# Moving one of the three rotary products of a fused attention kernel from VectorE to GpSimd

## The reference, cut to what matters

```python
def rotate_half(x):
    d = x.shape[-1] // 2
    return jnp.concatenate([-x[..., d:], x[..., :d]], axis=-1)
# NH = 16 heads of HD = 16; cos and sin of position x frequency
q, k = q * cos + rotate_half(q) * sin, k * cos + rotate_half(k) * sin
ctx = sdpa(q, k, v, causal=True)
```

## Time and profile before

| | |
|---|---|
| median of three runs | 522.23 us (522.04 to 524.18) |
| profiled execution | 521.07 us, of which the span is 518.9 us |
| granted TensorE clock, mean | 0.963 |
| PE busy | 435.7 us (84%) |
| DVE busy | 353.8 us (68%) |
| ACT busy | 257.0 us (50%) |
| POOL busy | 152.0 us (29%) |
| the cosine products, L1072 on DVE | 16, 10.9 us |
| the q adds, L251 on POOL | 16, 13.3 us |
| chain that ended last | PE 59%, DVE 18%, ACT 7%, issue 5%, DMA 5%, POOL 4% |

### The profile page before, as it was taken

One profiled execution on the slowest core, in us unless ns is written; L12 is line 12 of the kernel. 1 busy time (PEld: TensorE's weight loads), 2 busy tenths in 40 slices (PEclk: granted clock), 3 DMA queues, 4 the chain that ended last, 5 costly groups with the idle time before them and its releaser, 6 DMA issues.

```text
span 518.9 us, 10981 instructions
## 1 busy us (share of the span) xinstructions
PE 435.7 (84%) x3842; PEld 337.3 (65%) x3842; DVE 353.8 (68%) x804; ACT 257.0 (50%) x726; POOL 152.0 (29%) x268
## 2 busy tenths in 40 slices
PE   1098669997899999999999999999997986898992
PEld 1076538675577777776776776776866875676771
DVE  5934468797698698698699599699682650535543
ACT  0356456663554564464464564464451432655662
POOL 3585233113123123113114114013012103446542
PEclk9999958999999999999999999999997997999996
DMA  7587763633103103103103103001004001112111
GB/s 244 187 283 237 250 243 129 197 126 123 32 20 95 42 11 104 42 1 113 42 1 113 42 3 113 25 18 52 9 4 142 22 20 51 32 51 69 54 42 41
DMA packets 29492, 44.44 MB, mean 86 GB/s; under 512 B 4224, under 2 KB 22528, under 8 KB 29440
## 3 DMA queue, kind: packets, MB, share of 16 engines
q1 hardware_dynamic: 25792, 31.12, 18.4%
q0 software_dynamic: 3648, 12.62, 7.4%
HBM read 27.34 MB, written 16.38 MB: 84 GB/s over the span
## 4 chain that ended last, share of the span: by engine, by line
PE 59%; DVE 18%; ACT 7%; issue 5%; DMA 5%; POOL 4%; POOLq 0%; SPq 0%; ACTq 0%; DVEq 0%
PE xyz L1444 6%; PE xyz L1485 5%; DVE E L1094 4%; PE xyz L1471 4%; PE b_ps L1598 4%; DVE mx L1092 4%; PE b_ps L1361 3%; PE b_ps L1362 3%; PE b_ps L1363 3%; POOL x_rows L1277 3%; PE xyz L1648 2%; PE xyz L1361 2%; PE xyz L1362 2%; PE xyz L1363 2%; PE xyz L1553 2%
## 5 line engine op out<-in xcount | busy, mean ns | idle before, releaser
L1092 DVE TENSOR_REDUCE mx<-xyz 128x8 f32<-128x512 f32 x64 | 43.8, 684 | 13.9 <-PE xyz L1444 13.7
L1094 DVE TENSOR_TENSOR E<-xyz,mx 128x512 f32<-128x512 f32 x64 | 44.3, 692 | 2.2
L1444 PE MATMUL xyz<-kT,qT 32*64 32x128 f32 (+1 forms) x768 | 44.3, 333 | 1.7
L1471 PE MATMUL xyz<-cst,E 128*128 128x128 f32 x256 | 37.2, 283 | 5.7 <-ACT E L787 2.8
L1598 PE MATMUL b_ps<-w_gu_hi,ms_hi 128*128 (+2 forms) x90 | 38.0, 422 | 3.9 <-ACT ms_hi L811 3.9
L1314 POOL TENSOR_TENSOR mvar<-mss,pow_eps 128x1 f32<-128x1 f32 x17 | 3.2, 188 | 121.2 <-ACT m_sqr L803 119.2
L1471 PEld LDWEIGHTS xyz<-cst,E 128*128 128x128 f32 x256 | 28.7, 143 | 14.7 <-ACT E L787 6.2
L1485 PEld LDWEIGHTS xyz<-vb,kT 128*64 128x64 f32 x1024 | 32.4, 138 | 6.7 <-issue 6.5
L1485 PE MATMUL xyz<-vb,kT 128*64 128x18 f32 (+1 forms) x1024 | 35.7, 219 | 0.0
L1598 PE MATMUL b_ps<-w_gu_lo,ms_hi 128*128 (+2 forms) x90 | 34.5, 384 | 0.0
L251 POOL TENSOR_TENSOR qk<-E 128x256 f32<-128x256 f32 x16 | 13.3, 834 | 72.1 <-DVE E L1074 71.9
(11 more groups left out here) (273 smaller groups left out, 1251.5 us busy)
## 6 DMA issues: line engine op xcount, KB each, us to landing
qkv_rows<-qrow SPq DMA_DIRECT2D x18, 384.0 KB, 2.7
xq<-x_rows SPq DMA_DIRECT2D x18, 128.0 KB, 2.5
xm<-h_rows SPq DMA_DIRECT2D x17, 128.0 KB, 2.6
h_rows<-xm SPq DMA_DIRECT2D x17, 128.0 KB
x_sb<-in_x_dram SPq DMA_DIRECT2D x8, 256.0 KB, 2.8
E<-in_x_dram SPq DMA_DIRECT2D x2, 512.0 KB, 7.0
kT<-in_x_dram SPq DMA_DIRECT2D x2, 512.0 KB, 8.4
ctxT_a<-in_ctxT_dram SPq DMA_DIRECT2D x8, 128.0 KB, 2.3
```

Source lines behind the costliest of these rows:

```text
L1092: dve.tensor_reduce(mx[:, t, heads], s, AX.X, ALU.max).then_inc(max_ready, 1)
L1094: dve.tensor_tensor(E[t][:, b * 512:(b + 1) * 512].rearrange("p (h k) -> p h k", k=SEQ), s, mx[:, t, heads].unsqueeze(2).to_broadcast([P, ...
L1444: last = pe.matmul(xy[t][q, hp, o:o + w], qT[t][rows, c, q], kT[t][rows, (2 * c + b) * w:(2 * c + b + 1) * w], start=not masked, stop=True ...
L1471: last = pe.transpose(xy[t][:, a // 4, (a % 4) * P:(a % 4 + 1) * P], E[t][:, a * P:(a + 1) * P], ident)
```

## The change

`rope_q` on DVE no longer makes the cosine product. `rope_add` on POOL makes it, from the same gathered rows into the same 512 columns of `E[t]`, after waits for the gather and for the last reader of `E[t]` (or the table, for tiles 0 and 1), and posts the same `rope_a`. DVE still waits for `rope_a` ahead of the k add. The table `ORDER` is unchanged. With one line less in DVE's part, the lines behind L1066 move up by two, and by five more behind the new code: the turned products are L1071 and L1072 in the changed kernel, the cosine product is L1303.

```diff
@@ DVE, rope_q
                 if not first(n):
                     dve.wait_ge(S["cpT_psy"], tl(n, t) - 2)
                 qk = qkv_t[t][:, 0:2 * H].rearrange("p (h d) -> p h d", d=HD)
-                straight = E[t][:, 0:2 * H].rearrange("p (h d) -> p h d", d=HD)
                 turned = E[t][:, 2 * H:4 * H].rearrange("p (h d) -> p h d", d=HD)
...
-                dve.tensor_tensor(straight, qk, table(0, HD), ALU.mult).then_inc(S["rope_a"], 1)
                 dve.tensor_tensor(turned[:, :, 0:hd2], qk[:, :, hd2:HD], table(HD, HD + hd2), ALU.mult).then_inc(S["rope_b"], 1)
                 dve.tensor_tensor(turned[:, :, hd2:HD], qk[:, :, 0:hd2], table(HD + hd2, 2 * HD), ALU.mult).then_inc(S["rope_b"], 1)
                 dve.wait_ge(S["rope_b"], 4 * n + 2 * t + 2)
@@ POOL, rope_add
             def rope_add(n, t):
+                pool.wait_ge(S[f"ld_qkv{t}"], 16 * n + 16)
+                if first(n):
+                    pool.wait_ge(S["rope_ready"], 1)
+                else:
+                    pool.wait_ge(S["cpT_psy"], tl(n, t) - 2)
+                pool.tensor_tensor(E[t][:, 0:2 * H].rearrange("p (h d) -> p h d", d=HD), qkv_t[t][:, 0:2 * H].rearrange("p (h d) -> p h d", d=HD),
+                                   rope[:, 0:HD].unsqueeze(1).to_broadcast([P, 2 * NH, HD]), ALU.mult).then_inc(S["rope_a"], 1)
                 pool.wait_ge(S["rope_a"], tl(n, t))
                 pool.wait_ge(S["rope_b"], 4 * n + 2 * t + 2)
                 add_turned(pool, t, 0, S["qr_ready"])
```

## The result

The changed kernel takes 534.41 us, the median of four runs (532.39, 532.78, 536.05, 536.26), against 522.13 us for the kernel before (four runs, 521.28 to 524.18). The ratio is 1.0229, with a 95% interval of 1.0172 to 1.0285. It is 12.3 us slower, inside the range. The profiled execution took 536.05 us, which is 15.0 us over the one of before.

A forecast was written before the change was run, and what follows sets the result against it. At the rotation the chain was taken to run on PE, with DVE and POOL nearly late. Delays of 5.1 + 3.4 + 0.5 = 9.0 us gave 530.1 us for the profiled execution, 531.2 us predicted (1.7% slower), range 527 to 536 us.

The forecast's parts named there:

- Price of the product, 1.30 us: One 512-column cosine product on POOL takes 1.30 us, with 1.0 us as lower and 1.85 us as upper bound.
- Even tiles, W1 to W6, free: The even tiles' products hide in POOL's idle time ahead of the q add and cost nothing.
- Odd tiles, product behind the scatter: In W1 to W6 POOL's odd product waits behind the even tile's scatter; the k add starts 0.98 us later.
- 6 x 0.85 us: At the odd tiles of W1 to W6 the scores start 0.85 us late per pair; six pairs, 5.1 us.
- the q add ends 0.6 us after the k add does: Odd tiles, W1 to W6: POOL's q add ends last, at 195.43 us for tile 7, as before the change.
- the k add comes last: Rival: POOL's add gets in first, DVE's stands still; eight odd tiles lose some 0.3 us more each, 533.6 us; 15%.
- Tiles 2 and 3, 3.4 us: End of W0: tile 2's product waits behind the last q_sq; PE's q transposes of tile 3 start 3.4 us late.
- Tiles 0 and 1, 0.5 us: After the gather, DVE's turned products and POOL's cosine product add up instead of overlapping: half a microsecond.
- The clock, 7%: Rival: TensorE's clock falls after the idle time at tiles 2 and 3, stretching scores up to 3 us: 534 us; 7%.
- DVE is the bound (3%): Rival: DVE's 0.60 us saved per tile reach the end, 512.6 us, faster; 3%.
- POOL works past the scatter (5%): Rival: the scatter leaves POOL free, so the odd product starts once h2 is there: 524.5 us; 5%.

The follow-up runs named there:

- even half: Against the kernel before, the cosine product moved to POOL for the even tiles 4 to 14 only: 521.66 us, ratio 1.000.
- k first: The whole change plus one wait, so that POOL's q add starts only after DVE's k add is done: 537.53 us, ratio 1.0326.
- W0 alone: Against the kernel before, the product moved to POOL for tiles 0 to 3 only: 526.75 us, repeated on the third chip at 530.50 us, ratio 1.009.
- early products: The whole change with both cosine products of a pair placed ahead of the even tile's q add and scatter on POOL: 521.91 us, ratio 0.9999.
- both profiles of the changed kernel: Traces of the unaltered changed kernel: one from the first measurement (534.41 us), one from its rerun on the second chip (537.89 us).
- odd half: Against the kernel before, the product moved to POOL for the odd tiles 5 to 15 only: 542.98 us, ratio 1.0432.
- with that wait filled down to 0.24 us: Odd tiles 5 to 15 only, plus 13 identity transposes on PE per odd tile during the k add wait: 541.76 us, ratio 1.0299, third chip.

## Why the prediction was right

The direction, the place and the mechanism were right, and the time lay 3.2 us over the point. That it lay inside the range is in part luck: the profile was 18.5 us late at the first scatter of W7, and 3.1 us were given back behind the last stage that the change touches; without them the median would be some 3 us more, above 536. By its own steps:

- **Price of the product, 1.30 us.** 1300 ns in the group; 1.27 to 1.29 us where it runs alone.
- **Even tiles, W1 to W6, free.** Shown by the even half alone, ratio 1.000.
- **Odd tiles, product behind the scatter.** Shown by moving it (with tile 2's) ahead: ratio 0.9999. DVE's new idle time is 2.35 us (predicted 2.2), and the k add starts 204.25 - 9.56 - 193.43 = 1.26 us late (predicted 0.98). The 0.28 us between are small parts: h2 came 0.46 us sooner instead of 0.60 (200.32 - 9.56 = 190.76 against 191.22), the scatter took 1.31 us instead of 1.22, and the k add starts 0.10 us behind the product's end instead of 0.04.
- **The mis-sized term: 6 x 0.85 us.** It was 6 x 1.55 = 9.3 us. The step that failed is "the q add ends 0.6 us after the k add does". It ended 0.28 us ahead of it, and PE waited for the k add, not for the q add as forecast. In all eight k adds that waited for POOL's product, DVE took 0.98 us instead of 0.43, which is the rival "the k add comes last" that had 15%. The end of the later add was forecast well, 1.06 us behind the product's end (195.43 against 194.37), and was 1.08. What the forecast lacked is what PE has left to do behind it: with q last only the q transposes, with k last the k transposes ahead of them (205.29 and 205.73, 0.44 us). The scores start 206.28 - 9.56 - 195.39 = 1.33 us late, and their first group takes 0.82 us instead of 0.64, probably since the expansions are late too: 1.5 us. The rival had put the difference at 0.3 us a tile; against the forecast it was 0.7, of which 0.28 are the small parts above. Putting k first gains only 0.1 us, as shown there.
- **Tiles 2 and 3, 3.4 us.** The q transposes came 4.8 us late; W0 alone (with tiles 0 and 1) costs 4.7 us (2.1 to 7.4). Of the 1.4 us between the forecast and the q transposes, 0.47 are the product of tile 2, which started at 112.19 instead of 111.72, 0.55 the long k add of tile 2, and 0.36 the k transposes of tile 3, which now stand behind the last add (123.12 to 123.48).
- **Tiles 0 and 1, 0.5 us.** Of the changed kernel the transfer in the chain that ended last, which answers to the earlier trace rows, and behind it DVE and POOL in order of time, which answers to the earlier trace rows:

```profile
61.54 6.61 DMA qkv<-qkv_rows,slot_q
```

```profile
68.27 1.45 POOL L1303 TENSOR_TENSOR E<-qkv,rope 128x512 f32<-128x512 f32 x1 [0.25 <-POOL qk L251]
...
68.51 1.48 DVE L1072 TENSOR_TENSOR E<-qkv,rope 128x256 f32<-128x256 f32 x1
...
70.03 0.42 DVE L251 TENSOR_TENSOR qk<-E 128x256 f32<-128x256 f32 x1
```

The second turned product lasts 1.48 us instead of 0.42 while POOL's product runs. The gather landed at 68.15 us, and the k add came 1.88 us behind it; before it was 69.96 - 68.54 = 1.42 us. That is 0.46 us more. The forecast's sum gave 70.52 - 68.54 = 1.98 us and work side by side 1.36, so the times nearly add up. (The 0.13 us that the forecast took off that sum has no row.) In the trace the k add itself is only 0.07 us late, since the gather landed 0.39 us sooner. By the Trainium skill's rule of an exclusive lock on the shared port pair (SBUF — State Buffer, "SBUF: two separate sides") this has to be so, and the trace agrees in both directions here: DVE stands still beside POOL (1.48, 0.98 and, with the early products, 0.88 us) as POOL did beside DVE (0.92 us). It agrees nearly, not to the last tenth: the two adds at tile 7 take 1.00 us together (204.23 to 205.23), where one after the other they would take 0.72 + 0.43 = 1.15.

- **The clock, 7%.** It fell at tiles 2 and 3 in both profiles of the changed kernel, behind 2.83 and 2.85 us of idle PE time, which I had thought too little. In the first profile the scores of W2 to W6 ran at 1.00, those of W7 didn't (0.50 in the stretch from 373 to 375 us). What the falls add to the profiled execution of the changed kernel can be estimated from tile 3 to tile 5: 4.4 us less 1.5, that is 2.9 us for two. The kernel with k first, whose clock held there (measured in another set), needs 37.63 us for this step against 40.89, 3.3 us less. So this rival came true in part, beside the one on the k add, and the point of 531.2 us held neither.
- **DVE is the bound (3%); POOL works past the scatter (5%).** Both fell: the even half wins nothing, and the product started 0.03 us after the scatter's record ended (201.53 + 1.31 against 202.87).

By the parts, 9.3 + 4.7 = 14.0 us stand against 12.3 us measured, and the difference is within the interval of W0's part (2.1 to 7.4 us). The parts don't add up in general: the odd half alone (1.0432) costs more than the whole, since the even product then delays h2, PE waits longer, and behind most of these longer waits the clock fell.

Open: why in runs of one kernel the clock falls in one stage and not in another. The four runs of the changed kernel lie at 532.6 and 536.2 us; two or three falls more or less would do that (1.2 to 1.4 us each in a score phase). But only one of the four has a trace, and their mean clocks don't sort them (0.967 and 0.960 at 532.78 and 532.39 us, 0.954 and 0.962 at 536.05 and 536.26), so the cause is open. No kernel run here was faster than before; the even half and the order with early products tie with it.

## What to carry to other kernels

An idle engine isn't free at every place of its queue. Before moving work there, look at what stands ahead of it: here a scatter that waited for the very engine that was relieved. The same operation placed two steps earlier cost nothing, and the relief was worth nothing either, as the relieved engine only waited for the one on the chain. And two adds that one semaphore releases on VectorE and GpSimd are to be counted nearly as a sum (1.00 us here, where alone they take 0.72 and 0.43). Then ask which of them ends last, and what the engine that needs both has left to do behind that one.

## What the runs showed of the hardware that was not expected

- **Who gets in first.** Where POOL posts the semaphore on which both adds wait, its add started 0.02 to 0.03 us ahead of DVE's in all eight cases of the trace, took 0.72 or 0.73 us, and DVE's took 0.98 us. Where DVE's started 0.11 us ahead, in the other eight, DVE's took 0.42 or 0.43 us and POOL's 0.90 or 0.91.
- **Short idle times and the clock.** A 1.65 us wait preceded a fall to 0.50 in five of six stages of the odd half, and with that wait filled down to 0.24 us the scores ran at 1.00 (on another chip). But the length of the wait doesn't decide alone: at tile 5 of the odd half 1.64 us passed without a fall, in the first profile of the whole change one of six waits of 1.2 us was followed by one, and at tile 3 the kernel with k first had waits of 2.31 and 0.46 us and no fall. At tile 3 filling the wait took away the fall at 124 us and left the one at 134 us, which the first profile also had and the second hadn't.
- **Chips differ.** The kernel before took 519.53, 521.60 and 527.24 us on three of them. On the slowest, PE is idle ahead of groups of score products in every stage (0.87 us at L1456 above, 0.71 us in the W0-only kernel), which the profile puts down to its own earlier ones; no trace from the other chips shows it. Why is open. A time in microseconds can't be carried from one to the other. A ratio is safer, but not exact either: the whole change gave 1.0229 in the first measurement and, by the medians, 1.035 on the second chip.
